# Causal self attention in two pairs of heads: scores and maxima split, the order of the queues rewritten

## The reference, cut to what matters

```python
q = apply_rope(split_heads(x @ Wq + bq)); k = apply_rope(split_heads(x @ Wk + bk))
v = split_heads(x @ Wv + bv)
att = einsum('bhqd,bhkd->bhqk', q, k) / sqrt(16)
att = where(tril(ones(256, 256)), att, -1e10)
y = einsum('bhqk,bhkd->bhqd', softmax(att), v)
x = x + merge_heads(y) @ Wp + bp          # x is layernormed before the three products
...
x_q, w_q = mxfp4(layernorm(x)), mxfp4(weight)     # blockwise maximum, scale, clip, round
x = x + x_q @ w_q.T + bias
```

## Time and profile before

| | us |
|---|---|
| median of 3 runs (2195.12 to 2203.02) | 2199.34 |
| the profiled execution, whole | 2203.82 |
| its span, first to last instruction | 2202.0 |
| what lies around the span | 1.8 |
| stage with the change, first scores to last normalisation | 164.26 |

### The profile page before, as it was taken

How to read it: one execution, slowest core, us unless ns; L and a number is a source line. 1 busy time by engine, 2 the same in 40 slices (tenths; PEclk the granted TensorE clock), 3 DMA queues, 4 the chain that set the end, 5 groups by cost and what they waited for, 6 DMA issues and landing times. The chain is left out here.

```text
span 2202.0 us, 34851 instructions
## 1 busy us (share of the span) xinstructions
PE 1807.5 (82%) x13676; PEld 1104.1 (50%) x13676; DVE 1233.7 (56%) x3075; ACT 1025.5 (47%) x1381; POOL 759.8 (35%) x669
## 2 busy tenths in 40 slices
PE   5969999999999898888687877877766849888874
PEld 2434554454445444556466723544444437676653
DVE  5142424333332300364578379899999995557675
ACT  1457657756765687112131145555546521214442
POOL 6343324433542230000030027777878850110000
PEclk8989999999999999999967855878787669999897
DMA  6647555655756170000120001223132252000000
GB/s 143 118 105 127 117 109 109 117 119 113 122 109 128 56 125 38 1 2 1 58 70 1 14 1 44 79 59 87 51 86 66 58 184 86 1 1 1 1 6 15
DMA packets 78046, 150.01 MB, mean 68 GB/s; under 512 B 15464, under 2 KB 63144, under 8 KB 71464
## 3 DMA queue, kind: packets, MB, share of 16 engines
q1 hardware_dynamic: 64304, 101.80, 16.5%
q0 software_dynamic: 12768, 42.59, 12.7%
q10 hardware_dynamic: 792, 3.17, 0.4%
HBM read 93.59 MB, written 2.62 MB: 44 GB/s over the span
## 5 line engine op out<-in xcount | busy, mean ns | idle before, releaser
L571 ACT ACTIVATE P<-R 128x1024 f32<-128x1024 f32 x512 | 506.8, 1026 | 222.3 <-PE R L112 186.3
L112 PE MATMUL R<-QS,KST 100*128 100x256 bf16 x2048 | 297.0, 277 | 60.2 <-ACT P L571 53.5
L112 PEld LDWEIGHTS R<-QS,KST 100*128 100x128 bf16 x2048 | 170.0, 98 | 224.8 <-ACT P L571 120.9
L1797 POOL TENSOR_TENSOR ACC<-ACC,PM 128x4096 f32<-128x4096 f32 x22 | 195.2, 8872 | 1.8
L200 POOL TENSOR_TENSOR LNrs<-LNve,pk_const 128x2 f32<-128x2 f32 x36 | 25.3, 703 | 462.7 <-DVE LNve L196 462.5
L112 PE MATMUL R<-OV,QT 32*128 32x512 f32 x512 | 183.0, 802 | 0.0
L789 POOL DMA_DIRECT2D KST<-OV x300 | 144.5, 490 | 71.7 <-PE R L112 55.2
L112 PE MATMUL R<-P,VP 128*32 128x256 f32 x2304 | 156.1, 388 | 5.3 <-issue 5.0
L601 DVE CAST OV<-RT 128x512 bf16<-128x512 f32 x64 | 27.7, 432 | 217.2 <-ACT RT L116 130.0
L733 POOL CAST OV<-RT 128x512 bf16<-128x512 f32 x64 | 42.6, 665 | 266.5 <-DVE RT L604 266.5
L1787 POOL TENSOR_TENSOR SM<-SM,NG 128x1 f32<-128x1 f32 x30 | 79.3, 2644 | 147.5 <-DVE PM L1716 147.5
(11 more groups left out here) (370 smaller groups left out, 3559.0 us busy)
## 6 DMA issues: line engine op xcount, KB each, us to landing
KST<-OV POOLq DMA_DIRECT2D x276, 128.0 KB, 10.8
CT<-in_ctxP SPq DMA_DIRECT2D x40, 768.0 KB, 4.4
CN<-in_ctxn SPq DMA_DIRECT2D x60, 384.0 KB, 3.5
CT<-in_ctxT SPq DMA_DIRECT2D x64, 192.0 KB, 2.5
KST<-OV SPq DMA_DIRECT2D x84, 128.0 KB, 10.4
KST<-in_ctxP ACTq DMA_DIRECT2D x4, 768.0 KB, 9.4
QS<-x_q POOLq DMA_DIRECT2D x24, 128.0 KB, 5.4
pk_a<-in_pk_a SPq DMA_DIRECT2D x1, 3014.0 KB, 10.4
```

Of the source, the lines that this page charges most:

```text
L112: return e.matmul(o, l, r, start=st, stop=sp, skip_group_check=True)
L571: e.activation(P[(32 * p + k0) % 3][:, :], ring.at(("s", p, k0))[:, :], ACT.Exp).then_inc(*EX.up((p, k0)))
L1797: e.tensor_tensor(acc[:, :], acc[:, :], pm, ALU.add).then_inc(*G.up(("sum", p, h)))
```

## The change

```diff
-                return [(b, p) for p in (("q",), ("k", "v"), ("ks",), ("norm", "xt"))[u % 4]] if b < NB else []
+                return [(b, p) for p in (("q",), ("k",), ("ks", "v"), ("norm", "xt"))[u % 4]] if b < NB else []
...
-                def scores(u):
+                def scores(u, g):
...
-                    for j in range(4):
+                    if u > 0:
+                        e.wait_ge(*S.at(("ex", u - 1, g)))
+                    for j in (2 * g, 2 * g + 1):
                         rows = slice(32 * j, 32 * j + 32)
-                        if u > 0 and j % 2 == 0:
-                            e.wait_ge(*S.at(("ex", u - 1, j // 2)))
                         mm(e, SP4[j][:, 0:128], QT[rows, 0:128], KT[rows, 0:128], True, False)
-                    for j in range(4):
+                    for j in (2 * g, 2 * g + 1):
                         rows = slice(32 * j, 32 * j + 32)
                         mm(e, SP4[j][:, 128:384], QT[rows, 128:256], KT[rows, :], False, False)
-                    for j in range(4):
+                    for j in (2 * g, 2 * g + 1):
                         mm(e, SP4[j][:, 0:128], IDB[:, :], CMB[:, :], False, False)
                         ins = mm(e, SP4[j][:, 256:384], IDB[:, :], CMB[:, :], False, True)
-                        if j % 2 == 1:
-                            ins.then_inc(*M.up(("s", u, j // 2)))
+                    ins.then_inc(*M.up(("s", u, g)))
...
                 for u in range(NU + 1):
+                    if u < NU:
+                        scores(u, 0)
+                        scores(u, 1)
                     if product_at(u) is not None:
                         q_product(product_at(u))
-                    if u < NU:
-                        scores(u)
+                    for b, p in pieces(u):
+                        if p in ("q", "k", "ks"):
+                            piece(b, p)
                     if u > 0:
                         turn(u - 1)
                     for b, p in pieces(u):
-                        piece(b, p)
+                        if p == "xt":
+                            piece(b, p)
                     if u > 0:
                         weighted(u - 1)
+                    for b, p in pieces(u):
+                        if p == "v":
+                            piece(b, p)
...
                 for u in range(NU + 1):
-                    if u > 0:
-                        turned(u - 1, 0)
-                        turned(u - 1, 1)
                     if u < NU:
                         exp(u, 0)
+                        exp(u, 1)
                     if u > 0:
-                        turned(u - 1, 2)
-                    if u < NU:
-                        exp(u, 1)
+                        for n in range(3):
+                            turned(u - 1, n)
...
                 for u in range(NU + 1):
-                    for b, p in pieces(u - 1):
-                        if p != "norm":
-                            piece(b, p)
+                    if u < NU:
+                        maxima(u, 0)
+                    if u > 0:
+                        normalise(u - 1)
                     if u >= 6 and u % 4 == 2:
                         added(e, u // 4 - 1)
                     if product_at(u) is not None:
                         q_added(product_at(u))
+                    for b, p in pieces(u - 1):
+                        if p == "v":
+                            piece(b, p)
                     if u < NU:
-                        if u >= 2:
-                            e.wait_ge(*S.at(("ex", u - 2, 1)))
-                        for g in range(2):
...
+                        maxima(u, 1)
                         for job in quant(u):
                             quantise(*job)
                         for b, p in pieces(u + 1):
                             if p == "norm":
                                 piece(b, p)
-                        e.wait_ge(*S.at(("ex", u, 1)))
...
+                        for b, p in pieces(u):
+                            if p in ("q", "k", "ks"):
+                                piece(b, p)
```

More of the change, by code:

```diff
@@ L2232, in piece @@
                         ins.then_inc(*M.up(("v", b)))
-                def scores(u):
+                def scores(u, g):
                     b, tl = u // 4, u % 4
                     QT, KT = buf("QT", b)[:, tl, :], buf("KT", b)[:, tl, :]
-                    if tl == 0:
+                    if tl + g == 0:
                         e.wait_ge(*V.at(("q", b)))
                         e.wait_ge(*V.at(("kt", b)))
-                    if u == 0:
+                    if u + g == 0:
                         e.wait_ge(*G.at("cm"))
-                    for j in range(4):
+                    if u > 0:
+                        e.wait_ge(*S.at(("ex", u - 1, g)))
+                    for j in (2 * g, 2 * g + 1):
                         rows = slice(32 * j, 32 * j + 32)
-                        if u > 0 and j % 2 == 0:
-                            e.wait_ge(*S.at(("ex", u - 1, j // 2)))
                         mm(e, SP4[j][:, 0:128], QT[rows, 0:128], KT[rows, 0:128], True, False)
-                    for j in range(4):
+                    for j in (2 * g, 2 * g + 1):
                         rows = slice(32 * j, 32 * j + 32)
                         mm(e, SP4[j][:, 128:384], QT[rows, 128:256], KT[rows, :], False, False)
-                    for j in range(4):
+                    for j in (2 * g, 2 * g + 1):
                         mm(e, SP4[j][:, 0:128], IDB[:, :], CMB[:, :], False, False)
                         ins = mm(e, SP4[j][:, 256:384], IDB[:, :], CMB[:, :], False, True)
-                        if j % 2 == 1:
-                            ins.then_inc(*M.up(("s", u, j // 2)))
+                    ins.then_inc(*M.up(("s", u, g)))
                 def turn(u):
@@ L2500, in vector, with maxima, normalise @@
                     piece(b, p)
+                def maxima(u, g):
+                    if u >= 2:
+                        e.wait_ge(*S.at(("ex", u - 2, g)))
+                    ps = two(R[g][:, :])
+                    e.wait_ge(*M.at(("s", u, g)))
+                    for k in range(2):
+                        ins = e.tensor_reduce(buf("MX", u)[:, k, 2 * g:2 * g + 2], ps[:, :, parts[k]], AX.X, ALU.max, negate=True)
+                    ins.then_inc(*V.up(("mx", u, g)))
+                def normalise(u):
+                    e.wait_ge(*S.at(("ex", u, 1)))
+                    e.reciprocal(buf("SU", u)[:, :, :], buf("SU", u)[:, :, :]).then_inc(*V.up(("rc", u)))
+                    e.wait_ge(*V.at(("rc", u)))
+                    for k in range(2):
+                        part = buf("PS", u)[:, :, parts[k]]
+                        by = buf("SU", u)[:, k, :].rearrange("p (n o) -> p n o", o=1).broadcast_to(list(part.shape))
+                        e.tensor_tensor(part, part, by, ALU.mult).then_inc(*V.up(("sc", u, k)))
                 for u in range(NU + 1):
-                    for b, p in pieces(u - 1):
-                        if p != "norm":
-                            piece(b, p)
+                    if u < NU:
+                        maxima(u, 0)
+                    if u > 0:
+                        normalise(u - 1)
                     if u >= 6 and u % 4 == 2:
```

## The result

| | before | after |
|---|---|---|
| median, us (4 runs each) | 2198.47 | 2236.99 |
| lowest and highest | 2195.12, 2203.02 | 2236.09, 2237.34 |
| span of the profiled execution | 2202.0 | 2235.5 |
| first scores of the stage to the last normalisation | 164.26 | 202.58 |

The changed kernel is slower: ratio 1.0173, interval 1.0154 to 1.0192, 38.5 us. The two spans differ by 33.5, which is 38.32 in the 16 units, 1.95 behind them, and -6.77 ahead of the stage, where the code is the same and single executions differ (those of the kernel before by up to 8).

The account below looks back on a forecast made before the run. The prediction took the stage as bound by a loop of waits passing between engines, mostly DVE and PE. The longer loop's 21.2 us plus 6.4 for clock falls gave 27.6, so 2199.34 + 27.6 = 2227 us; range 2208 to 2242.

Parts of the forecast that it names:

- The loop: From one unit's first scores to the next one's, through DVE, ACT and PE: 9.94 us a unit, against 6.95 before.
- The price of a pair: Scores on PE: first scores of two heads to their first maximum take 1.37 us, as with four heads.
- the rival with cheap pairs: Scores of a pair at 0.9, 9.47 us a unit, and a warm clock: 2213 us; chance 0.15.
- The cover: Second pair's scores on PE hide behind DVE's normalisation; without that, up to 1.37 us a unit.
- signs of the change: What the trace should show if right: waits on PE, DVE and ACT, plain units' scores 9.9 us apart, last stretch losing most.
- 12 to 13 above all: Plain unit: scores start 9.9 us after the last one's, most likely in units 12 to 13; 6.95 before.
- four falls of the seven: TensorE's clock falls in four of seven units with PE idle 2.7 us, at 1.6 each: 6.4 us.
- The sums at full clock: Predicted lengths of the four stretches of four units: 39.8, 48.0, 51.0 and 46.6 us, together +21.2.
- the prediction's list: Units without a `q`, `k` or `ks` piece, where PE idles 2.7 us: 3, 7 and 11 to 15.
- the bound: Upper limit for clock falls: seven falls, 11.2 us, and as much as 4 more if both quantised products go cold.
- the forecast's own 2219 to 2233: Whole kernel: loop at 9.94 us a unit and some clock falls, 2219 to 2233 us; chance 0.53.
- the clock falls wherever it can: Rival on TensorE's clock: 21.2 + 11.2 + 4 = 36 us slower, 2236 us; chance 0.20.

Follow-up runs that it names:

- ACT's order alone: Old kernel with only ACT's queue changed, both exponentials ahead of all three transposed copies; ratio 1.0197 to before, median 2241.20 us.
- TensorE kept busy: Changed kernel plus products of constant weights into free tile `R[2]`, read by nobody, in eight units where PE would idle; 2226.31 us, ratio 1.0119 to before.

## Why the prediction came out as it did

**The loop was right.** "`scores(u+1,0)` stands behind `weighted(u-1)`" and "`maxima(u+1,1)` is queued behind the normalisation" is the chain of unit 12. Unit 4, which is nearly all at full clock, takes 10.18 against the 9.94 of the sum, with its `q` piece hidden. Pulling the next scores out from behind `weighted` gives back all, taking the copies from behind `exp(u,1)` 28, taking the normalisation out 21; ACT's order alone, put into the old kernel, makes a loss of the same size. These don't add up to the loss and need not: each opens the same ring at another place.

**The price of a pair was right**: 1.36 measured, 1.37 taken. Two heads take as long as four, so the rival with cheap pairs falls. **The cover was right**: the second pair starts 1.19 behind the first and is ready before the normalisation has ended; without it, in the old order, it costs 13. The Trainium skill's TensorEngine Tiling (Array Packing), Key Properties, says that a change of the tiling mode drains TensorE. The trace can't settle its price: the weight loads into `R` (scores, masks, pieces) stand idle, for nothing that the profile shows, 50 times and 18.2 instead of 31 times and 10.3, partly because such a wait lasts 0.65 at half clock and 0.33 at full clock. That this is the drain is not shown. In PE's own rows the masks follow the scores without idle time, and nothing of it shows on the loop.

**Most signs of the change came as listed**: weight loads of `weighted` wait for the third copy in 14 units, first maxima wait for PE 16 times, the wait for exponentials vanishes, ACT waits for second maxima, and the last stretch loses most. One did not: a plain unit was to take 9.9, "12 to 13 above all", and takes 11.93, which is the next point.

**The step that was mis-sized is the clock**: "1.6. I take four falls of the seven, 6.4". The sums at full clock were 39.8, 48.0, 51.0 and 46.6; the stretches took 41.13, 50.07, 56.46 and 54.92, which is 1.3, 2.1, 5.5 and 8.3 more, 17.2 in all, growing as the granted clock falls (0.93, 0.87, 0.83, 0.59). Five things were missed:

- There were more falls. Stretch by stretch of 1 us, the granted clock of the changed kernel falls seven times in the 16 units: in 3, 6, 7, 10 and 11, and twice in 14. Units 6 and 10 were not on the prediction's list, and the idle time by which it chose does not tell the cases apart: in unit 6 the clock fell behind 2.15 of standing still, in unit 11 with no single gap above 1.02 in that unit before it.
- A fall costs a unit 2.0 and not 1.6: in unit 12 scores to maximum is 2.30 instead of 1.37, third transposes to copy 1.15 instead of 0.69, `weighted` to scores 1.44 instead of 0.79. The transposes, 0.46, were left out.
- A fall was priced as an event. Two of the seven are a state: the one of unit 7 lasts 17 us, into unit 8, and the one of unit 11 lasts 34, through unit 12, where TensorE has 9.03 of work in 11.93, and most of 13.
- Filler runs at half clock too, and is then no longer hidden. In unit 8 the `q` piece takes 5.92 instead of 3.66, the transposes stand behind it on PE, and the unit takes 13.43; in unit 6 the `v` piece takes 3.59 instead of 1.9.
- The products run at half clock as well. Timeline of the changed kernel, these two pieces, the two quantised products and the output product of unit 13:

```profile
2068.38 3.59 PE L112 MATMUL B<-pk_a,OV 128*128 128x256 f32 x8
...
2087.60 5.92 PE L112 MATMUL R<-OV,pk_a 128*128 128x256 f32 x16
...
2115.89 3.68 PE L112 MATMUL B<-q_WT,q_XT 128*128 128x256 f32 x8 [2.57 <-DVE X L2556]
...
2163.80 5.39 PE L112 MATMUL B<-pk_a,YT 128*128 128x256 f32 x16
...
2174.57 3.40 PE L112 MATMUL B<-q_WT,q_XT 128*128 128x256 f32 x8 [2.57 <-DVE X L2556]
```

The quantised products take 1.97 at full clock and the output product 3.72: 1.71 + 1.43 + 1.67 = 4.8 more. The prediction kept the quantised products out of the sum and in the bound.

Of the 17.2, the run with TensorE kept busy shows 11. The rest is read from the trace and not tested by itself. Each step of the changed kernel that ran at half clock, against its time at full clock, gives 1.9 in units 3 and 4, 1.6 in 6, 1.1 in 7, 3.5 in 8, 1.7 in 10, 1.1 in 11, 2.0 in 12, 3.7 in 13, 2.5 in 14 and 0.9 in 15: some 20, an estimate, so that the other terms of the sums were together about 3 too high.

2236.99 lies in the range but above the forecast's own 2219 to 2233, and beside the rival "the clock falls wherever it can" (2236). That rival had seven falls too, but partly in other units and at other prices; that it came within 1 us is luck.

**The head start** was rightly refused for this order. With the next first scores issued early it is there, as that run's timeline shows, but that it pays is not shown: the 0.2% of that run has the move of `v` in it, which alone is worth 0.45%, and the stage takes 163.58 where `v` alone, without any split, gives 157.15. The Trainium skill's Perfetto Trace Analysis, Optimizing Scalar/DVE Operations, says that breaking up instructions may let work finish sooner where engines cause bubbles without being full. No run here bears that out: the split alone costs 13, the change 38.5, and the early scores only undo that loss.

## What to carry to other kernels

Work moved forward in one queue gains nothing if what it needs stands in another queue behind the end of the old unit: write down, for the first instruction of the next unit, everything that it stands behind on every engine, and close the loop before costing any part. Where the new loop leaves TensorE gaps, price the lower clock over every TensorE step of the loop and for as long as the gaps last, not once for each fall. And look at a bundle's parts singly: here a piece moved to another unit, worth 10 us alone, was part of a change that lost 38.

## What the runs showed that was not expected

- Products that nobody reads, 107 more records on TensorE in the stage (1147 against 1040), make the kernel 11 us faster: the stage's clock goes from 0.80 to 0.93.
- After its fall in unit 11 TensorE stayed at 0.50 through the whole of unit 12, with 9.03 us of work in 11.93; it rose only within the output product of unit 13, where the stretch of 2167 to 2168 has 0.89 and the next one 1.00.
- Score products of two heads take 0.92, and those of four side by side 0.94.
